# Two of the four first state decays of a core stage are made two slots later on ScalarE

## The reference, cut to what matters

```python
x = x + A(layernorm(x))    # Mamba block: projection, causal convolution, state scan, gate, FFN (GELU), layer norm
x = x + F(layernorm(x))    # experts: 8 heads pick one of 8192 experts each; gather, dot, GELU, weighted sum
x = x + B(layernorm(x))    # gated scan with 16 states: sigmoid gates, tanh, projection, layer norm
x = x + F(layernorm(x))    # the experts once more
```

```python
dA = exp(delta[t, d] * A[d, n])                       # the "decay" of state n
h  = dA * h + (delta[t, d] * u[t, d]) * B[t, n]
y[t, d] += h * C[t, n]
```

## Time and profile before

| | us |
|---|---|
| time, median of 3 runs | 1910.81 (1910.78 to 1912.81) |
| the profiled execution's own time | 1913.43 |
| its span, first to last instruction | 1911.7 |
| one iteration of the loop, decay to decay (1032.21 to 1138.76) | 106.6 |
| DVE, PE, ACT, POOL busy | 1679.5, 1567.6, 1482.6, 1363.5 |

### The profile page before, as it was taken

How to read it: one execution, slowest core, us unless ns; L and a number is a source line. 1 busy time by engine, 2 the same in 40 slices (tenths; PEclk the granted TensorE clock), 3 DMA queues, 4 the chain that set the end, 5 groups by cost and what they waited for, 6 DMA issues and landing times. The chain is left out here.

```text
span 1911.7 us, 24589 instructions
## 1 busy us (share of the span) xinstructions
PE 1567.6 (82%) x6042; PEld 849.4 (44%) x6042; DVE 1679.5 (88%) x4338; ACT 1482.6 (78%) x3125; POOL 1363.5 (71%) x1209
## 2 busy tenths in 40 slices
PE   6887788889899989899898989898898978776340
PEld 3342344445454545454554545454554545343120
DVE  6888979899999999999999999999999998944554
ACT  5666768889898989998898989898899977664320
POOL 1535546487887887878788877878778786877766
PEclk8899999999999999999999999999999999897555
DMA  6111202022323223232323232232323232333333
GB/s 155 61 45 30 70 25 75 23 79 87 94 84 90 86 83 93 75 105 78 96 83 97 80 96 84 69 108 75 98 82 98 83 91 75 86 113 99 98 92 93
DMA packets 84508, 159.43 MB, mean 83 GB/s; under 512 B 21096, under 2 KB 47104, under 8 KB 84288
## 3 DMA queue, kind: packets, MB, share of 16 engines
q0 software_dynamic: 49152, 134.28, 24.3%
q1 hardware_dynamic: 33952, 23.04, 4.1%
q10 hardware_dynamic: 1248, 0.34, 0.1%
HBM read 149.20 MB, written 8.39 MB: 82 GB/s over the span
## 5 line engine op out<-in xcount | busy, mean ns | idle before, releaser
L1623 POOL DMA_INDIRECT rows<-in_experts,index x1024 | 987.6, 964 | 335.7 <-issue 291.3
L1502 DVE TENSOR_TENSOR_SCAN hp<-dA,fed_ps 128x1024 f32<-128x1024 f32 x256 | 583.2, 2278 | 4.1 <-DVE fed_ps L1481 1.0
L844 PE MATMUL ysum<-hp,ident 128*128 128x512 f32 x1024 | 482.8, 616 | 3.3 <-POOL hp L1640 2.1
L1640 POOL TENSOR_TENSOR hp<-hp,c_row 128x1024 f32<-128x1024 f32 x112 | 264.4, 2360 | 160.4 <-ACT c_row L1146 129.8
L1481 DVE TENSOR_TENSOR fed_ps<-du,b_ps 128x1024 f32<-128x1024 f32 x256 | 313.6, 1225 | 35.7 <-PE b_ps L817 24.8
L1129 ACT ACTIVATE dA<-delta,decay 128x511 f32<-128x511 f32 x512 | 333.1, 711 | 9.6 <-issue 4.6
L844 PEld LDWEIGHTS ysum<-hp,ident 128*128 128x128 f32 x1024 | 202.5, 199 | 222.3 <-issue 198.0
L1064 ACT ACTIVATE rows<-rows,coef 128x128 f32<-128x128 f32 x896 | 272.8, 393 | 6.7 <-DVE coef L1366 6.7
L988 ACT ACT_TABLE_LOAD x207 | 265.6, 1283 | 8.6 <-PEq L550 5.0
L1359 DVE CUSTOM_DVE_ANT_0 rows<-rows,xn 128x128 f32<-128x128 f32 x1024 | 227.4, 286 | 34.8 <-DMA rows<-in_experts,index 34.2
L733 PE MATMUL bank<-rows,ident 128*128 128x256 f32 x896 | 208.6, 387 | 0.8
(11 more groups left out here) (218 smaller groups left out, 2201.2 us busy)
## 6 DMA issues: line engine op xcount, KB each, us to landing
rows<-in_experts,index POOLq DMA_INDIRECT x1024, 2.7
x_in<-in_x SPq DMA_DIRECT2D x16, 256.0 KB, 4.1
rows<-in_x SPq DMA_DIRECT2D x16, 256.0 KB, 5.5
x_shifted<-rows SPq DMA_DIRECT2D x16, 256.0 KB, 2.0
x_res<-x_shifted SPq DMA_DIRECT2D x16, 256.0 KB, 4.3
y<-x SPq DMA_DIRECT2D x16, 256.0 KB, 2.6
rows<-in_taps SPq DMA_DIRECT2D x1, 512.0 KB
rows<-in_wq_t SPq DMA_DIRECT2D x1, 512.0 KB, 5.0
```

The source lines that it names most:

```text
L844: mm = nc.tensor.matmul(ysum[:, j, :], ident[:], hp[:, BUFFER[k], j, :], start=(k == SUM_ORDER[0]), stop=(k == SUM_ORDER[-1]))
L1502: nc.vector.tensor_tensor_scan(flat, dA[:, n % NDA, :, :].rearrange("p a b -> p (a b)"), fed_ps[:].rearrange("p a b -> p (a b)"), 0.0, ALU ...
L1623: pool.indirect_dma_start(e.rows[:, t, h, :], None, A["experts"], bass.IndirectOffsetOnAxis(ap=e.index[:, t, h:h + 1], axis=0)).then_inc(e ...
L1640: pool.tensor_tensor(state, state, c_row[:, k % NCR, :].unsqueeze(1).to_broadcast([P, NH, T]), ALU.mult).then_inc(pool_read, 1)
```

## The change

At slot 0 ACT now makes only the decays of states 0 and 1. Those of states 2 and 3 are made at the head of slot 2, so behind the tanh, the experts' GELU and the `flip` copy of slots 0 and 1, and ahead of the slot's `ln`, `rs`, `outT` and `h1T`. The decays of states 4 and later stay where they were. No operation on data is added or dropped; table loads are issued wherever the set then has to change.

```diff
                 for slot in range(TURN):
                     n, part = divmod(slot, TURN // NS)
+                    if CORE in has and n == 0 and part in (0, 2):
+                        for k in range(2) if part == 0 else range(2, LEAD + 1):
+                            decays_of(k)
                     if CORE in has and part == 0:
-                        for k in range(LEAD + 1) if n == 0 else [n + LEAD] if n + LEAD < NS else []:
+                        for k in [n + LEAD] if 0 < n < NS - LEAD else []:
                             decays_of(k)
```

## The result

The changed kernel takes 1937.62 us (median of four runs, 1934.05 to 1946.78) against 1910.8 us for the kernel before on the same chip: 1.0142 times as long, 95% interval 1.0121 to 1.0163. It is slower by about 27 us; 18 were forecast (1929 us, with a range of 1924 to 1934). The profiled execution has a span of 1937.3 us against 1911.7, so 25.6 us are to be found in the trace. Executions of one kernel differ by some us: 23 runs of the kernel before on one chip lay between 1903.55 and 1918.31 us. Lines from 1138 on stand three lower than before: the read of `rr` on DVE, 1515 in the prediction, is line 1518 now.

A forecast was written before the change was run, and what follows sets the result against it. DVE was taken to set the loop's pace, with `rr` just in time. Even stages 7.3, odd stages 7.0 and stage 15 3.8 us sum to 18.1 us, on 1910.81 giving 1929 us, range 1924 to 1934 (chance 0.62).

The forecast's parts named there:

- The even stages: Stages 4, 5, 6, 8, 10, 12, 14: `ln` 1.22 us later, DVE loses 1.04 us each, 7.3 us in all.
- The wait for `rr`: DVE's line 1515 waits about 1 us in even, 1 to 2.5 us in odd loop stages, some 14 us.
- the odd ones: Stages 7, 9, 11, 13: line 1515 moves 1.04 us in 9, 2.45 in 11, mean 1.75; 7.0 us in all.
- the sum of the loop: Stages 4 to 14: 7.3 us from even and 7.0 from odd stages, the full delay of `rr` taken as loss.
- The rival of the slower clock: PE's clock falls in the longer wait before line 921: 0.8 us in eleven stages, 1934 to 1947 us; chance 0.12.
- Stage 15: Last stage: decays and a table load follow DVE's `coef`, `outT` and the waits behind it 3.8 us later.
- a drain of about the load's own length at each switch: ACT's table switches: by the skill page stage 15 would lose 1.4 us more, sum near 19.5 us; trace shows no drain.
- before stage 4: Stages 0 to 3: ACT waits for DVE's statistics there, so neither gain nor loss was taken.
- DVE made nothing up: Rival, behind line 1515: DVE's waits for `top` and `fed_ps` shrink, making up part; 1915 to 1924 us; chance 0.14.
- "Faster": Rival, head of stage: moved decays free in ACT's idle time, at most 4.7 us of PE's waits off, 1906 us; chance 0.05.
- "no change": Rival, at DVE's line 1515: the delay of `rr` finds slack on DVE, 1911 us; chance 0.07.

The follow-up runs named there:

- Runs 4: The changed kernel with DVE's read of `rr` issued one slot later (slot 5 instead of 4): 1941.88 us, ratio 1.015.
- 6: The kernel before with 2.56 us of needless table loads on ACT ahead of `ln` in stages 0 to 14, no decay moved: 1936.71 us, ratio 1.0139.
- Runs 1: The change made in stages 0 to 14 alone, stage 15 as in the kernel before: 1933.35 us, ratio 1.0098.
- 2: The change made in stage 15 alone, all other stages as in the kernel before: 1915.83 us, ratio 1.0013.
- Run 10: The changed kernel with the exponentials' table load moved ahead of the `flip` copy: 1920.32 us, ratio 1.0042.
- 11: The kernel before with the exponentials' table load ahead of the `flip` copy, without the change: 1914.15 us, ratio 1.0014.
- run 5: Against the changed kernel, only the fourth state's decays are moved (1.25 us instead of 2.50), in every stage: 1917.0 us, ratio 1.003.
- run 3: Against the changed kernel, decays of states 2 and 3 moved still later, behind `rr`, stage 15 as before the change: 1960.71 us, ratio 1.025.

## Why the prediction was right in kind and short in size

**The even stages, as worked out.** The tanh was to start 0.5 us earlier against the first decay and the `flip` hardly at all (0.07); it was 0.53 (5.79 for 6.32 us) and 0.00. `ln` was to come 1.22 us later and came 1.27 later. DVE was to lose 1.04 us and waits 0.8 or 0.9. In six of the seven stages counted there line 921 kept 1.10 us after a wait of 2.7 to 2.8 us.

**The wait for `rr`, 14.3 us forecast and 14.3 measured,** but not stage by stage: six stages (4, 5, 6, 10, 12, 14) at 0.8 to 0.9, five (7, 8, 9, 11, 13) at 1.6 to 2.1. Stage 8 had been counted as even; its wait is 0.9 longer than theirs because PE's clock fell there and line 921 took 2.04 us. The mean of the odd ones was 1.8 for 1.75, but stage 9, worked out as 1.04, waited 1.91, and stage 11, worked out as 2.45, waited 1.59. That the sums agree so well is in part luck.

**The step that failed is the sum of the loop.** It took the wait for `rr` as the whole loss of a stage. The loop lost 17.15 us. What came on top is above all the wait for `b_ps`, 4.3 us more, behind the falls of PE's clock some 70 us into the stage; 1.0 and 0.4 us more go to the scan and to `top`, and DVE waits 2.6 us less for `bits`. The prediction put the clock at nothing in its sum and left it to a rival. Runs 4 and 6 show that the wait for `rr` is a sign: take it away and the time stays, make ACT late by other means and it comes back.

**The rival of the slower clock came about in part,** and mostly where it was not looked for. It was priced behind the longer wait of line 921, at 0.8 us in each of eleven stages for 1938 us. There only two stages were slow, 7 and 8. Stage 8 beside stage 10, with the same wait:

```profile
840.17 2.04 PE L921 MATMUL bank<-outT,w_ff 128*128 128x512 f32 x2 [2.72 <-ACT outT L1163]
1055.65 1.10 PE L921 MATMUL bank<-outT,w_ff 128*128 128x512 f32 x2 [2.72 <-ACT outT L1163]
```

The other falls are those some 70 us into the stage, in ten stages instead of five. So 1937.62 us is near that rival's figure, but most of the loss in the loop is still the wait for `rr`.

**Stage 15, 3.8 us forecast, measured 5.2.** Wait and added work were right (8.88 against 8.8 us on PE). The price of the slower clock after such a wait, 1.35 us, was argued for the loop stages and left out where the wait was longest. The Trainium skill, page "ScalarE: Activation LUTs", section "What ACT_TABLE_LOAD costs", counts a drain of about the load's own length at each switch; by it, as an estimate, the 8.88 would have been some 10.2 (5.01 + 2.66 + 2.50). The measurement does not show that. The rest of the 6.9 us of stage 15 and the tail, 1.7, and the 1.56 us lost before stage 4, where I had taken nothing, were not tried by themselves. Of the 1.56, 0.75 us are lost ahead of the first decay of stage 0 (32.95 against 32.20 us), where the two kernels do not differ yet.

**What stays open.** Runs 1 and 2 together give 21 us, the change 27; their intervals cover the difference, and no run tells whether the last stage costs more behind a changed loop. Run 10's profiled execution, the slowest of its nine, has a span only 12.1 us shorter than the changed kernel's, though its loop is 13.7 us shorter (1165.55 us); in the timed runs the gain is nearer 19. By `ln`, earlier by some 0.5 us in even and 1.4 us in odd stages, it would be some 10 us in the loop. Why PE's clock falls in more stages of the changed loop is open too. It is no accident of one execution: in the profiles of runs 2 and 11, whose loop is that of the kernel before, the fall some 70 us into the stage is in the same five stages, and in run 1's, with the changed loop, it is in all eleven.

**Rivals.** DVE made nothing up at `top` (7.4 to 7.8 us) or `b_ps`; it waited 2.6 us less for `bits`. "Faster" and "no change" needed idle time on ACT ahead of `ln` for all 2.5 us; run 5 shows that the loop had room for 1.25 us a stage, and the change that it had not for 2.5.

## What to carry to other kernels

Work that fills an engine's wait for another engine is free only there: move it behind the wait and the whole queue behind it is late by as much as was filled. Do not price the first reader that waits as the cause; ask which engine lost time, and check with dead time of the same length in the same place. An engine at some nine tenths of a stage may have little to spare: here 2.56 us more on ACT in each stage cost 0.7 us for each us, in both places tried. And do not read a mean clock of a long stretch as "the clock held": 0.98 in both loops hid 20 us more at half speed.

## What was not expected of the hardware

PE's clock does not follow the length of the last wait alone. In the changed kernel line 921 took 1.10 us after a wait of 2.72 us in stage 10 and 2.04 us after the same wait in stage 8, 1.83 us after 3.53 us in stage 7 and 1.13 us after 3.60 us in stage 9. In stage 15, 5.01 us without a matmul made it 2.05 us in the kernel before, and 8.88 us in the changed kernel 2.04 us; there the granted clock then stayed at 0.50 for some 6 us. Some 70 us into stage 11 the waits of PE just before were the same in both kernels (0.82, 0.25, 0.52 and 0.40 us before; 0.80, 0.25, 0.52 and 0.40 after), and the clock fell only in the changed one. The spread between executions of one kernel goes with the clock as well: of those 23 runs of the kernel before, the fastest (1903.55 us) has a mean granted clock of 0.938 and the slowest (1918.31 us) 0.928. In run 3 two short waits (2.28 and 0.93 us) were followed by pairs of matmuls of 0.63 us, 0.39 at full speed. A table load of 1.28 us begins 0.02 us after the copy before it, and the copy ran equally under the table of the exponentials (1.02 us for the `flip` in run 10 and in the changed kernel).
